# Two bursts of constant products taken out ahead of the second layer's MLP

## What is computed

```python
h = _rms_norm(x, ln1_w)
q, kk, v = projections of h (16 query heads, 8 key/value heads), rotary on q and kk
attn_out = causal softmax attention over the 256 chosen tokens, @ wo
x1 = x + attn_out
h2 = _rms_norm(x1, ln2_w)
mlp = jax.nn.silu(h2 @ w_gate) * (h2 @ w_up) @ w_down
gated = gate * (x1 + mlp) + (1.0 - gate) * x
```

## Time and profile before

| what | value |
|---|---|
| median of 3 runs | 1220.93 us (1220.4 to 1221.81) |
| the profiled execution, its own time | 1222.0 us |
| its span, first to last instruction | 1219.7 us |
| TensorE busy | 1185.5 us, 97% of the span |
| mean granted TensorE clock | 0.996 of full speed |

### The profile page before, as it was taken

How to read it: one execution, slowest core, us unless ns; L and a number is a source line. 1 busy time by engine, 2 the same in 40 slices (tenths; PEclk the granted TensorE clock), 3 DMA queues, 4 the chain that set the end, 5 groups by cost and what they waited for, 6 DMA issues and landing times.

```text
span 1219.7 us, 19564 instructions
## 1 busy us (share of the span) xinstructions
PE 1185.5 (97%) x6770; PEld 1033.0 (85%) x6770; DVE 905.3 (74%) x2483; ACT 629.7 (52%) x1449; POOL 517.1 (42%) x468
## 2 busy tenths in 40 slices
PE   9999999999999999998999999999999998999996
PEld 8998989898989898987888888898888875567896
DVE  5777777868686778787798978777677768777633
ACT  5544545545545455556455444455454444559652
POOL 3535344444444444367444444354444356000154
PEclk9999999999999999999999999999999999999999
DMA  8343443434243434457343334342434396436652
GB/s 276 75 89 77 89 95 70 99 66 106 59 101 65 100 65 104 82 145 188 102 89 81 84 74 101 68 101 62 100 70 96 65 232 220 161 119 187 221 185 74
DMA packets 250868, 135.55 MB, mean 111 GB/s; under 512 B 191681, under 2 KB 224449, under 8 KB 250769
## 3 DMA queue, kind: packets, MB, share of 16 engines
q1 hardware_dynamic: 250352, 132.99, 43.4%
q0 software_dynamic: 416, 1.31, 0.3%
HBM read 79.20 MB, written 8.91 MB: 72 GB/s over the span
## 4 chain that ended last, share of the span: by engine, by line
PE 79%; DVE 9%; DMA 4%; ACT 3%; POOL 2%; issue 2%; SPq 0%; ACTq 0%; POOLq 0%; DVEq 0%
PE proj L1496 42%; PE y L1496 13%; PE o L1496 9%; PE s L1496 7%; DMA turned<-prob 3%; PE tp L1496 3%; PE proj L1504 2%; DVE arena L2022 1%; ACT arena L1799 1%; PE s L1504 1%; DVE works L2153 1%; DVE prob L2071 1%; DVE yacc L2108 1%; DVE prob L2073 1%; DVE s L2057 1%
## 5 line engine op out<-in xcount | busy, mean ns | idle before, releaser
L1496 PE MATMUL proj<-arena 128*128 128x256 f32 (+1 forms) x3504 | 642.1, 333 | 2.7 <-DVE arena L2022 2.6
L1496 PEld LDWEIGHTS proj<-arena 128*128 128x128 f32 x3504 | 530.8, 189 | 64.9 <-DVE arena L2022 6.5
L2385 POOL TENSOR_SCALAR arena<-turned 128x384 fp32r<-128x384 f16 (+1 forms) x256 | 279.8, 1097 | 434.1 <-DMA turned<-prob 375.6
L1799 ACT ACTIVATE arena<-proj 128x256 fp32r<-128x256 f32 (+1 forms) x256 | 124.6, 488 | 194.0 <-PE proj L1496 167.5
L2375 POOL TENSOR_TENSOR arena<-wraw,arena 128x1024 fp32r<-128x1024 f32 x73 | 176.0, 2414 | 103.5 <-ACT arena L1799 89.8
L1496 PE MATMUL y<-arena 128*128 128x512 f32 x816 | 211.5, 395 | 4.0 <-DVE arena L2022 2.8
L2022 DVE TENSOR_TENSOR arena<-proj,arena 128x256 fp32r<-128x256 f32 (+1 forms) x256 | 140.8, 553 | 79.9 <-ACT arena L1799 78.9
L1849 ACT ACTIVATE arena<-turned 128x384 fp32r<-128x384 f16 (+1 forms) x256 | 126.4, 495 | 108.0 <-DMA turned<-prob 106.4
L1496 PEld LDWEIGHTS y<-arena 128*128 128x128 f32 x816 | 149.2, 189 | 34.9 <-DVE arena L2022 3.8
L1496 PE MATMUL o<-arena 128*128 128x256 f32 (+2 forms) x966 | 171.7, 303 | 4.6 <-POOL arena L2385 1.3
L1496 PEld LDWEIGHTS o<-arena 128*128 128x128 f32 x966 | 149.4, 189 | 17.9 <-issue 2.5
(11 more groups left out here) (175 smaller groups left out, 980.9 us busy)
## 6 DMA issues: line engine op xcount, KB each, us to landing
wraw<-in_L_attn_Wv SPq DMA_DIRECT2D x16, 512.0 KB, 3.7
wraw<-in_L_attn_Wo SPq DMA_DIRECT2D x16, 512.0 KB, 4.0
wraw<-in_L_attn_Wq SPq DMA_DIRECT2D x15, 512.0 KB, 3.7
wraw<-in_L_attn_Wk SPq DMA_DIRECT2D x15, 512.0 KB, 3.8
yacc<-in_L_attn_hidden_states SPq DMA_DIRECT2D x16, 256.0 KB, 4.0
turned<-prob SPq DMA_TRANSPOSE x256, 2.8
y_dram<-yacc SPq DMA_DIRECT2D x16, 256.0 KB, 2.6
out<-works SPq DMA_DIRECT2D x16, 256.0 KB, 2.4
```

The lines of the kernel that those rows point to most:

```text
L1496: ins = e.matmul(out_ap, l[a], r[b], start=first and i == 0 and j == 0, stop=final and i == n - 1 and j == 2, skip_group_check=skip)
L1799: e.activation(dst, src, ACT.Copy).then_inc(*S_.inc(*name, "hi"))
L2385: e.tensor_scalar(strided(pT[1], js[0] * 3 * P + (i - js[0] + 1) * P, 2 * P, n, P), tT[i % 2][:, n:2 * n, :], 1.0 / PROB_SCALE, None, ALU. ...
```

## The change

It removes the last two entries of WARM, WARM[3] and WARM[4], with their entries in the order and their waits. The three bursts at the start of the program stay. No other line differs.

```diff
-WARM = (18, 6, 36, 44, 20)
+WARM = (18, 6, 36)
...
-V.wsplit.89.V V.av2s.1.7 D.wload.92 T.o2.1.7 S.wsplit.90.V V.wsplit.90.V T.warm.3 V.res.1 D.wload.93 S.wsplit.91.V
-G.res.1 V.wsplit.91.V V.resx.1 D.wload.94 S.wsplit.92.V T.resh.1 T.warm.4 S.resh.1 V.wsplit.92.V S.plnorm.1.0
+V.wsplit.89.V V.av2s.1.7 D.wload.92 T.o2.1.7 S.wsplit.90.V V.wsplit.90.V V.res.1 D.wload.93 S.wsplit.91.V
+G.res.1 V.wsplit.91.V V.resx.1 D.wload.94 S.wsplit.92.V T.resh.1 S.resh.1 V.wsplit.92.V S.plnorm.1.0
...
             job("resx", b)
-            if b == NB - 1:
-                hold("y", ("warm", 3), T_, "warm", 3, "made")
-                job("warm", 3)
             hold("o0", ("resh", b), V_, "resh", b, "lo")
             job("resh", b)
-            if b == NB - 1:
-                hold("y", ("warm", 4), T_, "warm", 4, "made")
-                job("warm", 4)
...
                     pe.wait_ge(*V_.at("const", "ones"))
-                    if key[0] >= 3:
-                        pe.wait_ge(*(T_.at("o2", 1, NKV - 1, "made") if key[0] == 3 else T_.at("resh", 1, "made")))
-                        pe.wait_ge(*freed("y", "warm", key[0]))
                     for _ in range(WARM[key[0]]):
```

## The result

| | before | changed |
|---|---|---|
| median of 16 runs each | 1221.63 us (1219.91 to 1223.45) | 1223.51 us (1222.27 to 1225.79) |
| ratio to before, 95% interval | | 1.0018 (1.0010 to 1.0025) |
| profiled execution, its own time | 1222.0 us | 1222.31 us |
| its span | 1219.7 us | 1220.1 us |
| its mean granted clock | 0.996 | 0.994 |

The change makes the kernel slower, by 1.9 us between the medians and by 2.2 us by the ratio (0.0018 x 1221.6), with an interval of 1.2 to 3.1 us. Zero lies outside that interval.

The account below looks back on a forecast made before the run. TensorE, busy 97% of the span, was taken as the bound, its clock deciding. Bursts removed 0, later effects 0, low clock on transposes and gate-up 1.3 us: 1220.93 us became 1222.2 us, range 1220.3 to 1223.8 us.

Parts of the forecast that it names:

- Within 0.2%: Whole kernel: the changed time cannot be told from before, within about 2.4 us; chance 0.84.
- the side above it: Whole kernel: slower by over 0.2%, that is by more than 2.4 us; chance 0.13.
- Steps 1 and 2: Between attention and gate-up: removing 3.92 us of burst products, and their waits, is worth 0 on the chain.
- Step 3: Ahead of the transposes: TensorE idle 3.86 us, so the clock falls 2.4 to 3.3 us after the last attention product.
- Step 4, the price per low microsecond: Transposes and gate-up under a low clock: 0.45 us for the transposes, 0.46 us per low microsecond of gate-up.
- Step 4, how much of gate-up lies in the low stretch: Start of gate-up: 0.33 to 3.4 us low; with the transposes 0.60 to 2.0 us in all, middle 1.3 us.
- Step 5: From gate-up to the end: a later start causes no new wait and nothing is won back, 0 us.
- two stretches on gate-up: Start of gate-up: clock low over 2 x 3.4 us, costing 3.6 us, giving 1224.5 us; chance 0.09.
- No fall: Passage ahead of gate-up: the clock stays up and nothing changes, 1220.9 us; chance 0.13.
- a clock that hangs: The MLP: clock stays low for its 62.6 us, costing 29 us, giving 1250 us; chance 0.01.

Follow-up runs that it names:

- the second profile: The changed kernel, unaltered, timed and profiled once more against the kernel before: 1224.23 us (8 runs), ratio 1.0024 (1.0014 to 1.0035).
- the last kernel of the section before: Against the kernel before, three more bursts (20, 24, 12) added elsewhere and the burst of 20 ahead of gate-up out: 1220.48 us, ratio 0.9994.
- the first group: No change: 35 runs of the kernel before, timed on one chip beside four of the experiment kernels, median 1220.91 us.

## Why the prediction was right or wrong

**The direction and the mechanism were right, the size was not.** 1222.2 us was forecast, 1.3 us more than before; the measured median, 1223.51 us, lies inside the range of 1220.3 to 1223.8 us. Of the 1.3 us between forecast and median 0.7 us is the kernel before itself, whose median was 1220.93 us in 3 runs and 1221.63 us in these 16. The effect by the ratio is 2.2 us, and 2.9 us (0.0024 x 1222) when timed again, against the 1.3 us of the sum. "Within 0.2%" holds for 1.0018 and not for 1.0024, so the effect sits on that line, and the 0.13 given to the side above it was too little. The sums of the prediction hold, but for a trifle: the lower end of the range takes 0.6 us off where the three runs give 0.53 us.

**Steps 1 and 2** (the bursts and their waits are worth 0): right. Without the burst of 20 gate-up starts 1.40 us after the transposes (1139.89 - 1138.49), as it did with it, and the kernel with that burst alone removed is not told from before.

**Step 3** (the clock falls 2.4 to 3.3 us after the last attention product): a fall was right, its time roughly. The changed kernel's last attention product ends at 1130.52 + 3.12 = 1133.64 us, and the clock is down by 1138.0 us, 4.4 us later; it is still up at 1137.6 us, 4.0 us later. In the second profile the last attention product ends at 1132.18 + 3.11 = 1135.29 us and the clock is down by 1137.3 us, 2.0 us later. So two falls read from one trace do not bound the delay.

**Step 4, the price per low microsecond** (0.46 us): right. The changed kernel lost 2.13 us over 4.9 low us of gate-up, the second profile 2.51 over 5.8, the one-element products 2.39 over 5.5: 0.43 each. With the half burst it is 2.16 over 4.9, 0.44, and in the kernel that keeps only the burst of 20 it is 1.02 over about 2.35 by the timeline, again 0.43. The half that the Trainium skill charges (page "TensorE: Matmul & The Clock Gate", section "HAM oscillation — how this bites in real kernels") would be a little too much here, because the products at the upper level take 0.123 us and not the half of 0.218. The transposes: 0.45 us was the price if wholly covered; 0.46 us in the second profile, 0.18 us in the first, none with the one-element products.

**Step 4, how much of gate-up lies in the low stretch: this is the step that failed.** Its ends were 0.33 and 3.4 us, the second taken from the one low stretch of 3.4 us in mid-kernel, and the middle was taken for want of a reason. Measured: 4.9 us in the changed kernel, 5.8 us in the second profile, 5.5 and 4.9 us in the profiles of the one-element products and of the half burst. In the sum's own terms, gate-up was given a loss of 0.15 to 1.55 us, 0.85 us in the middle, and lost 2.13 and 2.51 us. The stretch in the earlier trace rows had TensorE busy for all of its 3.4 us and was over then. Here the first part of the low time holds only the transposes and a pause, and the clock did not come back until gate-up had run for about 5 us. Why it stayed down longer is not shown. That little work fell in the first part of the stretch is the likely reason, and the profile of the kernel that keeps only the burst of 20 fits it: there the burst filled the pause, and the stretch was 3.4 us long. But two low stretches of mid-kernel speak against a plain rule. One of the changed kernel was over after 3.4 us, though TensorE was busy for 2.61 of 3.20 us of it only (first line); one of the last kernel of the section before lasted 6.8 us, though TensorE was busy for 5.92 of 6.40 us of it (second line). The prediction had seen that more than half of the new stretch would be idle, and drew from it only that neither end was nearer; it should have put a longer stretch than the one of the earlier trace rows among the ends.

```profile
1008.40:1011.60 3.20, 2.61 (x7) 1.72 (x6) 2.81 (x13) 1.09 (x2) 2.62 (x7) 0.50 1.05 401
...
1014.70:1021.10 6.40, 5.92 (x16) 3.74 (x15) 4.39 (x11) 3.16 (x6) 3.84 (x10) 0.50 0.47 165
```

With 4.9 us on gate-up and 0.18 us on the transposes its sum would have been 0.18 + 0.46 x 4.9 = 2.4 us, with 5.8 us and 0.45 us it would have been 3.1 us; the two profiles show 2.13 + 0.18 = 2.3 and 2.51 + 0.46 = 3.0 us.

**Step 5** (no second loss, nothing won back): right, 48.13 against 48.14 us.

**The rivals.** The one for slower, two stretches on gate-up, had a chance of 0.09 and was the nearest to what happened: its deciding point, 4.3 us of low clock on gate-up, was passed by 0.6 and 1.5 us. Its price of 3.6 us was too high, as it had 6.8 us on gate-up itself. No fall, and a clock that hangs, were not seen in any of the five profiles in which the burst of 44 was out, cut or empty.

Over many executions a rough count agrees. It is an estimate, since the executions of before are those of another group and low stretches elsewhere are counted too. A mean clock of c means 2 x (1 - c) of the span at the lower level. The 16 executions of the changed kernel have a mean of 0.9937, the 35 of before in the first group 0.9961, or 15.4 and 9.5 us low. Of the 5.9 us more, 4.9 / 6.8 lie on gate-up as in the profile: 4.2 us, which at 0.43 is 1.8 us, with the transposes' 0.2 us 2.0 us, against the 1.9 to 2.2 us measured. For the second timing, beside its own group, 17.7 and 9.0 us low give 8.7 us more, of which 5.8 / 10.2 or 4.9 us on gate-up: 2.1 us, with the transposes' 0.46 us 2.6 us, against 2.2 us between the medians and 2.9 us by the ratio.

## What to carry to other kernels

Where a chain leaves TensorE for some microseconds and comes back to it for a long dense run, what matters is not only the gap but the microseconds of dense work that start under a low clock: price them as low time on the dense run, and allow for a low stretch longer than the shortest one in the trace, above all where little work falls in its first part. Two profiles of one kernel had 4.9 and 5.8 us of it on the dense run, so one profile is one draw. Products that nobody reads can hold the clock up, if there are enough of them and they end before the next real product is due; here 2.63 us of them in a gap of 3.9 us did, a burst of half the size did so at best in some executions, and one placed late, after the clock had a chance to fall, delayed what it was meant to help. Such an effect of 0.2% shows in the stretch of one profile and not in its span, and needs dozens of runs to be timed.

## What was not expected of the hardware

- Low stretches came in lengths of 3.4, 6.8 and 10.2 us. In the changed kernel and in those with one-element products and with half the burst they ended only after 4.9 to 5.8 us of dense gate-up, whereas in the earlier trace rows one ended after 3.4 us of work.
- 64 products of one row by one column, 1.24 and 0.64 us of busy time in the record, did not hold the clock, where the 64 full ones (2.63 and 1.29 us) and the 44 full ones alone did. Their number is not what counts. As 22 full products, 1.30 us busy, did not hold it in the profile either, the busy time may be, and whether the size of a product matters beyond it was not tested.
- The kernel before loses its clock near 1009 to 1023 us in some executions and not in the same place in others, and once for 10.2 us in an execution whose time, 1220.91 us, is the median of its group. What that stretch cost is not shown: VectorE, GpSimd and ScalarE carry much of the chain there, but six products in it that take 2.94 us together, and 1.65 us at the upper level (at 1022.10 us in the first profile), are on the chain too.
